# Experts work on tiles of their own tokens, scattered to and gathered from lists in DRAM

## The reference

```
x = layernorm(x + attention(x))
shared = (silu(x @ sw1) * (x @ sw2)) @ sw3
probs = softmax(x @ rw + rb);  w, idx = top_k(probs, 2);  w = w / sum(w)
gates = sum over the two picks of w * one_hot(idx, 8)
h = silu(x @ ew1[e]) * (x @ ew2[e]);  eout[e] = h @ ew3[e]        for every expert e of 8
routed = sum over e of gates[e] * eout[e]
out = layernorm(x + shared + routed)
```

## Time and profile before

| what | us |
|---|---|
| three executions | 280.47, 283.03, 579.79 |
| median | 283.03 |
| span of the profiled execution, first to last instruction | 277.7 |
| prologue, to the first expert matmul | 0 to 35.3 |
| loop of 72 steps | 35.3 to 270.7 |
| after the last matmul of y | 7.0 |
| TensorE busy | 246.3 |
| VectorE busy | 202.8 |
| ScalarE busy | 155.3 |
| GpSimd busy | 153.4 |

### The profile page before, as it was taken

How to read it: one execution, slowest core, us unless ns; L and a number is a source line. 1 busy time by engine, 2 the same in 40 slices (tenths; PEclk the granted TensorE clock), 3 DMA queues, 4 the chain that set the end, 5 groups by cost and what they waited for, 6 DMA issues and landing times.

```text
span 277.7 us, 3718 instructions
## 1 busy us (share of the span) xinstructions
PE 246.3 (89%) x1134; PEld 180.8 (65%) x1134; DVE 202.8 (73%) x470; ACT 155.3 (56%) x260; POOL 153.4 (55%) x136
## 2 busy tenths in 40 slices
PE   3699378899999979999999969999999979999991
PEld 1297255687886755777787735777886746777770
DVE  1698779978659749987458768986558768575655
ACT  2568257378934437377944347367944445654640
POOL 6304704574898543566658653575758545575522
PEclk9979775999999979999999999999999999999997
DMA  7990000000000000001000000001000000010001
GB/s 146 403 361 4 4 0 0 1 2 0 0 0 2 2 0 0 0 2 39 0 4 0 0 0 0 2 0 38 5 0 0 2 0 0 0 41 0 1 0 38
DMA packets 6499, 7.63 MB, mean 27 GB/s; under 512 B 384, under 2 KB 5120, under 8 KB 6480
## 3 DMA queue, kind: packets, MB, share of 16 engines
q1 hardware_dynamic: 6080, 6.92, 7.5%
q10 hardware_dynamic: 400, 0.49, 0.6%
HBM read 6.35 MB, written 1.05 MB: 27 GB/s over the span
## 4 chain that ended last, share of the span: by engine, by line
PE 66%; DVE 23%; issue 4%; DMA 3%; ACT 1%; POOL 1%; ACTq 1%; DVEq 0%; POOLq 0%
PE gate_bank L507 6%; PE y_bank L507 5%; PE gate_bank L510 5%; PE gate_bank L508 5%; PE up_bank L507 5%; PE y_bank L508 5%; PE y_bank L510 5%; PE up_bank L510 5%; PE up_bank L508 5%; PE s_bank L499 4%; PE m_bank L428 4%; PE m_bank L461 4%; DVE x L871 4%; DMA xg<-selectors 3%; PE t_bank L442 2%
## 5 line engine op out<-in xcount | busy, mean ns | idle before, releaser
L1116 POOL TENSOR_TENSOR hlo<-h,hhi 128x512 fp32r<-128x512 f32 x69 | 90.3, 1311 | 68.7 <-ACT hhi L711 68.6
L706 ACT ACTIVATE sil<-gate_bank 128x512 f32<-128x512 f32 x72 | 42.9, 596 | 52.4 <-PE gate_bank L510 52.0
L955 DVE TENSOR_TENSOR h<-sil,up_bank 128x512 f32<-128x512 f32 x72 | 48.5, 679 | 20.3 <-ACT sil L706 13.7
L711 ACT ACTIVATE hhi<-h 128x512 fp32r<-128x512 f32 x72 | 44.9, 624 | 4.4 <-DVE h L955 4.4
L1121 POOL TENSOR_TENSOR xglo<-xg,xghi 128x512 fp32r<-128x512 f32 x24 | 32.3, 1346 | 22.7 <-ACT xghi L717 22.7
L507 PE MATMUL gate_bank<-x2hi,up_hi 128*128 128x512 f32 x72 | 32.4, 450 | 0.0
L933 DVE TENSOR_TENSOR xg<-x2T,s_bank 128x512 f32<-128x512 f32 x32 | 21.8, 680 | 14.3 <-PE s_bank L499 14.1
L507 PE MATMUL y_bank<-hhi,down_hi 128*128 128x512 f32 x72 | 30.6, 425 | 0.0
L510 PE MATMUL gate_bank<-x2lo,up_hi 128*128 128x512 f32 x72 | 29.4, 408 | 0.0
L508 PE MATMUL gate_bank<-x2hi,up_lo 128*128 128x512 f32 x72 | 29.0, 403 | 0.0
L508 PE MATMUL y_bank<-hhi,down_lo 128*128 128x512 f32 x72 | 28.6, 397 | 0.0
(11 more groups left out here) (160 smaller groups left out, 449.7 us busy)
## 6 DMA issues: line engine op xcount, KB each, us to landing
up_f<-up_w SPq DMA_DIRECT2D x2, 768.0 KB, 8.5
down_f<-down_w SPq DMA_DIRECT2D x2, 384.0 KB, 9.6
xr<-x_rows SPq DMA_DIRECT2D x1, 768.0 KB, 12.9
out<-result SPq DMA_DIRECT2D x3, 256.0 KB, 2.3
xT<-x_cols SPq DMA_DIRECT2D x2, 256.0 KB, 6.3
up_f<-up_w SPq DMA_DIRECT2D x1, 512.0 KB, 6.9
xT<-x_cols SPq DMA_DIRECT2D x1, 512.0 KB, 11.1
kM<-masks ACTq DMA_DIRECT2D x1, 272.0 KB, 6.3
```

The costliest lines, as they stand in the source:

```text
L706: act.activation(sil[:, t % 2, :], gate_bank[t % 2][:, :], ACT.Silu).then_inc(silu_done, 1)
L711: act.activation(hhi[:, at % RING, :], h[:, at % 2, :], ACT.Copy).then_inc(hhi_done, 1)
L955: dve.tensor_tensor(h[:, t % 2, :], sil[:, t % 2, :], up_bank[t % 2][:, :], ALU.mult)\
L1116: pool.tensor_tensor(hlo[:, at % RING, :], h[:, at % 2, :], hhi[:, at % RING, :].bitcast(F32), ALU.subtract).then_inc(hlo_done, 1)
```

## The change

The tokens are handled in two halves of 1,024 (two chunks each). The router's two picks give each token two (expert, rank) positions: `rank` on TensorE counts, with a triangular matrix and ones, how many earlier tokens of the half picked each expert, and `places` on VectorE makes a row number of it in a list in DRAM that has room for 1,152 rows for each expert. GpSimd then writes each 128-token tile of x2 twice with an indirect DMA (`scatter`), 16 for a half. `make_table` works out from the counts which expert each of 23 tiles of 128 rows belongs to and where its rows begin (8 experts, 16 full tiles' worth of picks, 7 for the tiles that are not full); `find` works out where each token's two results will lie. SyncE fills the end of each list with zeros at addresses that it reads from the table, and loads the tiles, two to a pair; TensorE reads from the table which weights a tile takes. Both read the table into registers (`values_load_multi_w_load_instructions`: 31 values on SyncE, 23 on TensorE, for each half).

A pair of tiles is turned on TensorE (`turn_rows`), split, and multiplied with rows as the stationary side and 512 weight columns (gate and up together) as the moving side, into the two banks of `gu`, which is not doubled. h is turned (`turn_hidden`), split on ScalarE and VectorE, and multiplied down: hi with 256 columns (hi and lo weights side by side), lo with 128. ScalarE copies y out, GpSimd adds its two parts, SyncE stores 256 rows to `y_list`. When all tiles of a half are stored, GpSimd gathers for each 128 tokens their two rows (`gather`, 16 indirect DMAs for a half), and VectorE multiplies them by the two gates and adds them to x2 plus the shared expert's result (`combine`), with rows on partitions, takes the statistics and scales.

The steps (`ITERS` = 32) are: shared expert of chunks 0 and 1 (0 to 3), 12 pairs of half 1 (4 to 15), shared expert of chunks 2 and 3 (16 to 19), 12 pairs of half 2 (20 to 31). The prologue now holds attention and router of chunks 0 and 1, the rest of chunks 2 and 3 lies beside steps 0 to 14. Half 1's gathers lie beside steps 20 to 27, half 2's come after all steps. kM, vbd, mx, mrow, prob and esink are doubled. The weights have one layout, expert by expert; ScalarE makes x2hi from PSUM; `gsel`, `xg` and their splits are gone.

The diff, cut to its core:

```diff
-WEIGHT_LOTS = [(0, 1), (1, 3), (3, 6), (6, 9)]
+LIST = HALF_TOKENS + P
+R_TILES = 2 * HALF_TOKENS // P + EXPERTS - 1
+PAIRS = (R_TILES + 1) // 2
+WEIGHT_LOTS = [(8, 9), (0, 2), (2, 5), (5, 8)]
+S0, S1, R0, S2, S3, R1 = 0, 2, 4, 4 + PAIRS, 6 + PAIRS, 8 + PAIRS
+ITERS = R1 + PAIRS
...
+            for hf in range(HALVES):
+                sp.wait_ge(table_done, hf + 1)
+                fill_ends(hf)
+                row = fetch_table(hf, T_ROW, T_ROW + R_TILES)
+                for n in range(PER_HALF * hf, PER_HALF * (hf + 1)):
+                    sp.wait_ge(scattered[n], 16 * 2 * ROWT)
+                sp.wait_ge(filled[hf], 16 * EXPERTS)
...
+                for p in range(PAIRS):
+                    if p + XRING < PAIRS:
+                        load_rows(first + p + XRING, row)
+                    if p >= XRING:
+                        store_rows(first + p - XRING)
...
+            def up_routed(i, pair, w):
+                pe.wait_ge(xhi_done, pair + 1)
+                pe.wait_ge(xlo_done, pair + 1)
+                after(pe, h_done, i)
+                for q in range(width(pair)):
+                    at = w[2 * (pair % PAIRS) + q]
+                    hi = w_cut[:, bass.ds(at + UP_HI, CT)]
+                    lo = w_cut[:, bass.ds(at + UP_LO, CT)]
+                    pe.matmul(gu_half[q], rows_hi, hi, start=True, stop=False)
+                    pe.matmul(gu_half[q], rows_lo, hi, start=False, stop=False)
+                    mm = pe.matmul(gu_half[q], rows_hi, lo, start=False, stop=True)
+            def down_routed(i, pair, w):
...
+                for q in range(width(pair)):
+                    for k in range(2):
+                        pe.matmul(y_bank[:, q * WIDE:(q + 1) * WIDE], hhi[:, i % RING, cols],
+                                  w_cut[:, bass.ds(at, 2 * D)], start=q == 0 and k == 0, stop=False)
+                        mm = pe.matmul(y_bank[:, q * WIDE:q * WIDE + D], hlo[:, i % RING, cols],
+                                       w_cut[:, bass.ds(at, D)], start=False,
+                                       stop=q == width(pair) - 1 and k == 1)
+            for i in range(ITERS + 2):
+                if i in (R0 - 1, R1 - 1):
+                    w_next = fetch_weights(int(i > R0))
+                if i + 1 < ITERS and pair_of(i + 1) is not None:
+                    turn_rows(pair_of(i + 1))
+                if i < ITERS:
+                    if shared_of(i) is not None:
+                        up_shared(i, *shared_of(i))
+                    else:
+                        up_routed(i, pair_of(i), w)
+                beside(i, 0)
+                if 0 <= i - 1 < ITERS and pair_of(i - 1) is not None:
+                    turn_hidden(i - 1, pair_of(i - 1))
+                beside(i, 1)
+                if i >= 2:
...
+            for i in range(ITERS + 2):
+                if i + 1 < ITERS and pair_of(i + 1) is not None:
+                    rows_low(pair_of(i + 1))
+                beside(i, 0)
+                if i < ITERS:
+                    hidden(i)
+                beside(i, 1)
+                if 0 <= i - 1 < ITERS and pair_of(i - 1) is not None:
+                    hidden_low(i - 1, pair_of(i - 1))
+                beside(i, 2)
+            for n in range(PER_HALF, CHUNKS):
+                for j in range(ROWT):
+                    combine(n, j)
+                    if j == 3:
+                        scale2(n, 0, 2)
+                scale2(n, 2, ROWT)
...
+            def scatter(n, first, last):
+                pool.wait_ge(pos_done, n + 1)
+                pool.wait_ge(x2_done, ROWT * (n + 1))
+                for j in range(first, last):
+                    for k in range(2):
+                        pool.indirect_dma_start(
+                            x_list[n // PER_HALF][:, :],
+                            bass.IndirectOffsetOnAxis(ap=pos[:, n, k, j:j + 1], axis=0),
+                            x2[:, n * ROWT + j, :], None).then_inc(scattered[n], 16)
+            def gather(n, j):
+                if here == 0:
+                    pool.wait_ge(found_done, hf + 1)
+                    for r in range(YRING):
+                        pool.wait_ge(y_stored[r], 16 * y_stores(r, PAIRS * (hf + 1)))
+                for k in range(2):
+                    pool.indirect_dma_start(
+                        z[:, 2 * here + k, :], None, y_list[hf][:, :],
+                        bass.IndirectOffsetOnAxis(ap=found[:, n, k, j:j + 1], axis=0)).then_inc(z_in[here], 16)
...
+            weights_low(0)
+            rstd1_of(0)
+            weights_low(1)
+            x2_low(0)
+            rstd1_of(1)
+            weights_low(2)
+            x2_low(1)
+            scatter(0, 0, ROWT)
+            weights_low(3)
+            scatter(1, 0, ROWT)
...
+            for n in range(PER_HALF, CHUNKS):
+                for j in range(ROWT):
+                    gather(n, j)
+            for n in range(PER_HALF, CHUNKS):
+                for i in range(2):
+                    rstd2_of(n, 2 * i, 2 * i + 2)
```

1555 lines of the change are left out of this document (919 added, 636 removed).

## The result

The changed kernel takes 303.4 us (median of four executions, 301.3 to 305.7). The kernel before took 280.5, 283.0 and 284.7 us beside it; a fourth execution took 579.8 and stands apart. The change makes the kernel 1.075 times as long, with a 95% interval of 1.065 to 1.086. 269 us were forecast, with a range of 243 to 296. The profiled execution is the slowest of the four, 305.7 us with a span of 303.8; the profile before spans 277.7. Ratios and intervals here are taken from the executions of a kernel that agree, so they can differ by up to 0.009 from the quotient of two medians, and none is given where too few agreed.

A forecast was written before the change was run, and what follows sets the result against it. The prediction took TensorE to set the pace before the change. It added stage costs, prologue through end, to 267.8 us, took 1.3 off each of two single pairs for a span of 265.2, and forecast 269 us, range 243 to 296.

The forecast's parts named there:

- Its own sum: Whole kernel: stage costs added up give a span of 265.2 us and a time of 269 us; chance 47%.
- rival (a): Steps 0 to 3 and half 1: attention fits into waits, saving 13 and 14 us, 242 us in all; chance 23%.
- (b): Scatters and gathers: VectorE holds GpSimd's address writing; indirect DMA at 1.8 us gives 293, at 2.34 gives 319; chance 22%.
- (c): Routed pairs: register addresses break TensorE's stream, 0.7 us a pair over 24 pairs, +17, 286 us, no change; chance 8%.
- the weight splits meet both scalings, +5.3: Prologue: GpSimd's weight splits (3.8 and 5.4 us) hold VectorE's scalings of both chunks, adding 5.3 us.
- twelve circles 39.6 ... 28.0 ... 67.6: Half 1: twelve pair circles, 39.6 us, plus VectorE's remaining work on chunks 2 and 3, 28.0, make 67.6 us.
- 4 x 3.3 = 13.2, and 2 of register loads: Shared steps 16 to 19: four steps of 3.3 us plus 2 us of TensorE's bare register loads before step 20.
- The 36%: Whole kernel: the rows left after the change are 36% of the rows before.
- The indirect DMA: Scatters and gathers on GpSimd: 1.3 us each, sixteen a half; forecast wrong if under 0.9 or over 1.7 us.
- The circle of a pair: Routed pairs: undoubled gate and up banks make the next matmuls wait until h has been read, 3.3 us a pair.
- The end: After the last h: 6.5 us to the last store, sixteen bare gathers 20.8, roots and dependent VectorE work 11.7; 39.0 us.
- The 620 and 3100 ns: Scatters: the skill page's GpSimd-issued DMA, alone and beside two-port VectorE; by it sixteen scatters take 50 us, not 21.

The follow-up runs named there:

- e4b: Changed kernel with tile t taking the weights of expert t // 3, so TensorE loads no registers (result differs): 300.0 us, ratio 1.078.
- e2b: Changed kernel with the split of the last three experts' weights moved on GpSimd behind both chunks' scatters of half 1: 305.0 us, ratio 1.085.
- e8: Changed kernel with lists as in e1b, last split behind the first 2 scatters, chunk 3's scatters in one go, roots sooner: 299.5 us, ratio 1.068.
- e11: Changed kernel with GpSimd's last weight split behind 4 scatters and not before VectorE's picks of chunk 1 are done: 306.6 us, ratio 1.097.
- e13: Changed kernel with the last weight split moved from GpSimd to VectorE, behind its picks of chunk 1: 298.9 us, ratio 1.060.
- e7: Changed kernel with unread matmuls of zeros on TensorE in the prologue, before steps 1 and 2 and in steps 11 to 19: 301.6 us, no interval.
- e5: Changed kernel with TensorE's matmuls that weigh the values of chunks 2 and 3 issued twice: ratio 1.118.
- e6: Changed kernel with one more VectorE reduction before each of the eight scalings of attention's output in steps 5 to 8: ratio 1.096.
- e9: Changed kernel with TensorE's rankings of chunks 2 and 3 one step later and ScalarE's tangents and x2 copies behind the step's Silu: 302.6 us, no interval.
- e1b: Changed kernel with half 2's lists zeroed at the start and its row numbers read before half 1's last two y stores: 295.5 us, ratio 1.054.
- e10: Changed kernel with e1b, e9, e11, chunk 3's scatters in one go, roots sooner, half 2's first eight tiles loaded before the last stores: 290.4 us, ratio 1.035.
- e14: All repairs (e10) with the split on VectorE and chunk 3's last two scatters behind the sum of pair 9: 287.1 us, ratio 1.012.
- e3b: Changed kernel with chunk 2's reciprocal roots issued on GpSimd ahead of the last two of the sixteen final gathers: 298.8 us, ratio 1.066.
- e15: e14 with unread filling matmuls of zeros on TensorE in steps 13 to 19: median 3.1 us higher than e14, ratio 1.035.
- e12: e10 with chunk 3's two shared steps put behind the last pair of half 2: 293.7 us, ratio 1.045.

## Why the prediction was wrong

Its own sum was 38.6 us short of the span. Neither rival (a) nor the mechanism of (b) was what happened: the one rival that said "slower" had the wrong cause, an indirect DMA of 1.5 us or more. The waits that (c) put at 0.7 us a pair were 0.12 (e4b).

**The prologue, "the weight splits meet both scalings, +5.3".** This step failed in size and place. I read the earlier trace rows as something that happens to scalings. It happened to small operations too: `picked` took 3.41, four scalings 2.53 in place of 1.11, the table's operation 5.67. Over their usual times these are some 10 us and not 5.3. Two copies of 32 columns took 2.54 us at 23.06 (0.36 elsewhere), 2.2 more; they met not a split but GpSimd's addition of a bias, which has no term in the sum. Not all of VectorE's work was held. Beside the same kind of split, operations that read PSUM were not (keys at 49.56 took 1.52, as in the earlier trace rows), and neither were a reciprocal (0.20 at 35.90) and stream transposes (0.70 at 36.35), whose one input lies in SBUF. That it is the last split that held the table's operation is shown by e2b, e8 and e11, where it moved and held another operation each time, and by e13, where it was gone. The rest of the 9.8 us was not taken apart. VectorE waited 3.2 us for the router matmuls of chunk 1 and 4.1 for its ranks; with fillings ahead of it the second wait was 2.7 (e7).

**Half 1, "twelve circles 39.6 ... 28.0 ... 67.6".** The step that failed is that VectorE's attention was added to the circle and TensorE's was left out. A pair alone takes TensorE 3.0 of its 3.25 us, and steps 5 to 8 add transposes and weighings of two chunks, so that 28.7 us hold 27.4 busy, while VectorE, forecast at over 80%, is busy 43.25 of 77.7. e5 against e6 shows it. In steps 10 to 15 nobody is full: Silu, tangent, picks and ranking stand in one another's way, which is worth 2.2 to 5.5 us of 38.0 (e9). What part TensorE's low clock has there (3.3 us between profiles of the same lists) is open.

**Shared steps 16 to 19, "4 x 3.3 = 13.2, and 2 of register loads".** It counted TensorE's loads and not SyncE's queue. For half 1 I had listed SyncE's loads and fills, and they were covered; for half 2 I did not ask what they stood behind. SyncE's own list was 6.6 us of the 14.8 (e1b). The order on GpSimd, which sets when the scatters and the last sum are done, together with rows loaded ahead of the last stores, was 1.6 more (e10, e14: steps 16 to 20 from 20.3 to 18.7, in all 8.2 gained). What is left over the forecast (6.6 us) was not taken apart; in e14 the matmuls of steps 18 and 19 run at half the clock (0.43 us apart from 194.24 and from 199.70), those of steps 16 and 17 at the full one.

**Smaller slips.** Rival (a) takes 13 us off four shared steps, where the sum holds only three behind the first h. Rival (c) makes 0.7 us of four addresses at 0.43, which are 1.7, less the 0.2 that the circle already has. The 36% are the experts' rows alone; with the shared ones it is 43%. The profiled execution took 1.9 us outside its span, not 4.

**What held.** The indirect DMA, the step on which rival (b) stood. The groups by shape:

```profile
L1437 POOL DMA_INDIRECT x_list<-x,pos x32 | 31.1, 973 | 8.9 <-issue 8.9
L1453 POOL DMA_INDIRECT w_raw<-y_list,found x32 | 30.5, 955 | 10.9 <-issue 7.9 <-DMA y_list<-w_raw 2.4
```

One lasts 0.96 us and one is issued every 1.26, forecast 1.3. The circle of a pair, forecast at 3.3, read from starts of h in half 2:

```profile
230.41 0.69 DVE L1211 TENSOR_TENSOR h<-sil,gu 128x512 f32<-128x512 f32 x1 [1.16 <-ACT sil L887]
233.67 0.69 DVE L1211 TENSOR_TENSOR h<-sil,gu 128x512 f32<-128x512 f32 x1 [0.46 <-ACT sil L887]
236.92 0.69 DVE L1211 TENSOR_TENSOR h<-sil,gu 128x512 f32<-128x512 f32 x1 [0.44 <-ACT sil L887]
```

3.25 us, with TensorE's up matmuls starting 0.24 us behind the end of each h. Half 2 came out right by its circle, and by the sizes in it: 256 and 128 columns together cost 0.23 us, forecast 0.22. The end, 39.0 forecast, is 41.3: the roots' order is named in the forecast and was worth 2.4 (e3b).

In the changed kernel no scatter or gather was longer than 1.2 us, so what the prediction feared of rival (b) didn't happen. In e13, e14 and e15, where VectorE's split (a `tensor_tensor` with both inputs in SBUF) lay beside a scatter, that DMA took 2.39 to 2.40 us and ended with the split. The Trainium skill (SBUF — State Buffer, Who interferes with whom) reports a `tensor_copy` that stalled a GpSimd-issued DMA and a `tensor_tensor` that did not. These three runs differ from the second half of that, and the measurement decides. The 620 and 3100 ns that the prediction takes from this page stand in its section "A bandwidth-pool intuition that's wrong".

## What to carry to other kernels

Cutting the work of the busiest engine by a fifth lengthened this kernel: nothing covered the other engines' waits any more. Where a change takes the bound away, sum every engine in every stage anew, the former bound too, and write down for each queue what stands ahead of the first thing that the next stage waits for: that list alone was 6.6 us here. In these profiles a long GpSimd tensor operation stopped VectorE's copy, cast, `tensor_scalar` and `tensor_tensor` operations on SBUF down to 8 numbers, also over several GpSimd operations in a row; reciprocals, reductions, transposes and whatever read PSUM went on, and GpSimd's roots of 4 numbers, 1.0 us long, held nothing (`lead` 0.17 at 55.31). So moving such an operation in GpSimd's list only moves the hold (e2b, e8, e11). Put it where VectorE waits or reads PSUM, or give it to VectorE (2.7 us for 5.4 in e13).

## What was not expected of the hardware

- Stalls of up to 8.5 us in which VectorE or ScalarE or both wait for a result of TensorE that its record shows as finished. The profiles of the changed kernel and of e1b to e5 have none, those from e6 on all do, e6, e7, e11 and e13 with the changed kernel's lists in half 2. They lie around steps 0 and 1 (e13 has a second one there, 5.5 us of ScalarE's, up to 89.3), in steps 16 to 18, in steps 20 to 23, and with e9's edit in steps 14 and 15 as well. The cause is open.
- The eight fills of SyncE, 4.0 us in the changed kernel, took 5.6 to 6.3 (e10, e11, e12) and 12.1 to 13.1 us (e8, e13, e14, e15). Scatters beside them are not enough to explain it, since the fills took 4.1 us beside an unbroken row of scatters in e2b. In e8 and e13 VectorE's stall before h0 falls into the same stretch (78.2 to 90.3 us in e8). Whether the two belong together is open, and so is the cause.
- Fp32r matmuls of 256 and of 128 columns come every 0.23 us as a couple, and those of 128 every 0.11: half of the 0.22 of fp32.
- A register load costs about 0.09 us (23 in 2.1, 8 in 0.8), so a list of them is an item of the sum.
